# A decoder layer's long convolution: the diagonal products in three split parts, the taps split once and loaded as three arrays, the last addition on GpSimd

## What is computed

```
kv[i,j,l]  = ctx[i,l] * ctx[j,l]                       (l = 0..511, 36 pairs i<=j)
y[i,j,l]   = sum over m<=l of taps[h,l-m] * kv[i,j,m]  + D[h] * kv[i,j,l]
out[j,l]   = sum over i of y[i,j,l] * q[i,l]           (q = normalised x, transposed)
```

## Time and profile before

| | us |
|---|---|
| median of 3 runs (2049.78 to 2053.88) | 2050.71 |
| the profiled execution | 2049.21 |
| its span in the profile | 2047.4 |
| PE busy in the span | 1961.0 (96%) |
| DVE busy | 1565.9 (76%) |
| ACT busy | 929.3 (45%) |
| POOL busy | 781.7 (38%) |
| granted TensorE clock, mean | 0.991 |

### The profile page before, as it was taken

The page is one execution under the profiler, slowest core; times in us unless marked ns, Lnnn a source line. Parts: engine busy times, 40 slices in busy tenths (PEclk is TensorE's granted clock), DMA queues, the critical chain, the costliest instruction groups (busy, mean ns, idle before and its releaser), DMA issues.

```text
span 2047.4 us, 44848 instructions
## 1 busy us (share of the span) xinstructions
PE 1961.0 (96%) x15500; PEld 1607.5 (79%) x15500; DVE 1565.9 (76%) x5012; ACT 929.3 (45%) x3481; POOL 781.7 (38%) x883
## 2 busy tenths in 40 slices
PE   6899999999999989989999999999998999999899
PEld 6788888888888867778888888888886677777687
DVE  5777777777777767667777777777776899999887
ACT  4554545555455544445555455545553222222233
POOL 4444433334333323323333232233331554555454
PEclk8999999999999999999999999999999999999999
DMA  5156111111111221111111111111114633332243
GB/s 209 42 131 138 60 56 53 53 73 53 53 63 63 84 87 60 63 42 53 53 53 53 53 53 56 60 53 53 53 52 152 173 98 87 90 90 85 98 147 121
DMA packets 71538, 162.20 MB, mean 79 GB/s; under 512 B 6656, under 2 KB 15232, under 8 KB 71184
## 3 DMA queue, kind: packets, MB, share of 16 engines
q1 hardware_dynamic: 62720, 142.48, 20.7%
q0 software_dynamic: 3840, 8.39, 2.2%
q10 hardware_dynamic: 4752, 8.46, 1.1%
HBM read 108.96 MB, written 50.41 MB: 78 GB/s over the span
## 4 chain that ended last, share of the span: by engine, by line
PE 76%; DVE 15%; issue 4%; ACT 3%; POOL 1%; DVEq 0%; DMA 0%; ACTq 0%; POOLq 0%
PE banks L528 21%; PE banks L590 15%; PE banks L543 9%; PE banks L1131 8%; PE banks L567 8%; PE banks L553 5%; PE banks L1337 4%; PE banks L521 4%; DVE terms L1163 2%; DVE m L854 2%; DVE pr L878 2%; DVE banks L1177 2%; DVE banks L1173 1%; ACT pr L664 1%; DVE terms L1180 1%
## 5 line engine op out<-in xcount | busy, mean ns | idle before, releaser
L664 ACT ACTIVATE pr<-pr,mx 128x128 f32<-128x128 f32 x1024 | 398.9, 391 | 419.7 <-DVE mx L878 419.7
L739 POOL TENSOR_TENSOR m<-m,rope_sb 128x512 f32<-128x512 f32 x160 | 206.9, 1293 | 522.3 <-ACT m L651 522.3
L528 PE MATMUL banks<-xTh,wh 128*128 128x256 f32 x1280 | 378.2, 295 | 2.9 <-DVE xTl L838 1.4
L528 PE MATMUL banks<-xTl,wh 128*128 128x256 f32 x1280 | 364.7, 285 | 0.0
L528 PE MATMUL banks<-xTh,wl 128*128 128x256 f32 x1280 | 364.4, 285 | 0.0
L1131 PE MATMUL banks<-kv,tap 128*128 128x288 f32 x1280 | 323.9, 410 | 12.7 <-DVE res L1187 10.9
L1131 PEld LDWEIGHTS banks<-kv,tap 128*128 128x128 f32 x1280 | 238.1, 190 | 98.1 <-issue 36.5
L528 PEld LDWEIGHTS banks<-xTh,wh 128*128 128x128 f32 x1280 | 248.1, 194 | 5.5 <-issue 2.7
L528 PEld LDWEIGHTS banks<-xTl,wh 128*128 128x128 f32 x1280 | 248.3, 194 | 0.0
L528 PEld LDWEIGHTS banks<-xTh,wl 128*128 128x128 f32 x1280 | 247.8, 194 | 0.0
L887 DVE TENSOR_TENSOR den<-ac,es 128x4 f32<-128x4 f32 x256 | 53.0, 207 | 251.8 <-ACT es L667 251.6
(11 more groups left out here) (110 smaller groups left out, 3840.1 us busy)
## 6 DMA issues: line engine op xcount, KB each, us to landing
tap<-padded_taps SPq DMA_DIRECT2D x64, 256.0 KB, 3.3
kk<-in_ctxt SPq DMA_DIRECT2D x64, 192.0 KB, 3.4
x_in<-in_x SPq DMA_DIRECT2D x16, 512.0 KB, 3.8
xt_split<-xTh SPq DMA_DIRECT2D x16, 512.0 KB, 2.6
xt_split<-xTl SPq DMA_DIRECT2D x16, 512.0 KB, 3.6
xb<-in_x SPq DMA_DIRECT2D x16, 512.0 KB, 4.5
factors<-in_factors POOLq DMA_DIRECT2D x8, 1024.0 KB, 8.6
x_part_rows<-x SPq DMA_DIRECT2D x16, 512.0 KB, 3.0
```

What stands on the lines that cost most here:

```text
L528: last = pe.matmul(bank[:, h * T:(h + 1) * T], w[:, n, c, h * P:(h + 1) * P], a[:, s, c, :], start=(c == 0 and i == 0), stop=(c == KD - 1 ...
L664: act.activation(pr[:, s, a, cols], pr[:, s, a, cols], ACT.Exp, bias=mx[:, s, i:i + 1], scale=-1.0, accum_out=ac[:, s, i:i + 1])
L739: pool.tensor_tensor(m2[:, s], m2[:, s], rope_sb[:, 1 if i == 0 else 0, 1:3], ALU.mult).then_inc(sin_ready, 1)
```

## The change

The four diagonal matmuls of a unit become twelve of type float32r, on split operands; the six below the diagonal stay float32. This holds from unit 2 on (`split(u)`); units 0 and 1 stay as they are. The taps are split once, during the attention, into a high and a low part, and DRAM scratch holds three arrays (whole, high, low). A unit loads three tap arrays: the whole one without its last block (128 x 384), and high and low (128 x 512 each). kv's first block is split in the unit, the high part by ACT, the low part by POOL. DVE's last addition goes to POOL. PE now waits for `one_added` in place of `res_ready`, DVE for `res_ready` of unit u-2. The buffer `pr` of the attention moves into the shared arena, where the convolution's high and low taps later lie.

```diff
     def load(sp, u):
         bg, h, s = where(u)
         wait(sp, kv_ready, u - 1)
         sp.dma_start(kk[:, s], ctx_in[bg, h]).then_inc(kk_landed[s], 16)
         wait(sp, conv_done, u - 1)
-        sp.dma_start(tap[:, s], bass.AP(tensor=pad_dram.tensor, offset=h * PADW, ap=[[1, P], [1, D]]))\
-          .then_inc(tap_landed[s], 16)
+        whole = D - P if split(u) else D
+        sp.dma_start(tap[:, s, 0:whole], diagonals(0, h, whole)).then_inc(tap_landed[s], 16)
+        if split(u):
+            for i, part in ((1, tap_hi), (2, tap_lo)):
+                sp.dma_start(part[:, s].bitcast(F32), diagonals(i, h, D)).then_inc(tap_landed[s], 16)
...
+    def diagonals(i, h, columns):
+        return bass.AP(tensor=pad_dram.tensor, offset=(i * CH + h) * PADW, ap=[[1, P], [1, columns]])
...
     def first_loads(sp):
-        sp.wait_ge(tap_out, 16)
+        sp.wait_ge(tap_out, 48)
...
+    def pairs_high(act, u):
+        act.wait_ge(kv_ready, u + 1)
+        act.copy(kv_hi[:, u % 2], kv[:, u % 2, 0, :]).then_inc(kv_hi_ready, 1)
+
+    def pairs_low(pool, u):
+        pool.wait_ge(kv_hi_ready, u - 1)
+        pool.tensor_tensor(kv_lo[:, u % 2], kv[:, u % 2, 0, :], kv_hi[:, u % 2].bitcast(F32),
+                           ALU.subtract).then_inc(kv_lo_ready, 1)
+
+    def last_sum(pool, u):
+        n, s = CD * BG, u % 2
+        pool.wait_ge(one_added, u + 1)
+        wait(pool, res_placed, u - 1)
+        pool.tensor_tensor(res[:, s], terms[:, s, :, n:2 * n], terms[:, s, :, 2 * n:3 * n], ALU.add).then_inc(res_ready, 1)
+
     def gpsimd(pool):
-        for u in range(2, NCU):
-            pairs(pool, u)
+        for u in range(NCU):
+            if u + 2 < NCU:
+                pairs(pool, u + 2)
+                pairs_low(pool, u + 2)
+            last_sum(pool, u)
...
         for u in range(NCU):
             if 1 <= u < NCU - 1:
                 fetch(act, u + 1)
+            if u + 2 < NCU:
+                pairs_high(act, u + 2)
             place(act, u)
...
     def products(pe, u):
         s = u % 2
-        pe.wait_ge(tap_landed[s], 16 * (u // 2 + 1))
+        pe.wait_ge(tap_landed[s], 16 + 48 * (u // 2))
         pe.wait_ge(kv_ready, u + 1)
-        wait(pe, res_ready, u - 1)
+        wait(pe, kv_lo_ready, u - 1)
+        wait(pe, one_added, u - 1)
         for d in range(KD):
+            block = slice(d * P, (d + 1) * P)
             for c in range(d, KD):
-                last = pe.matmul(y[:, s, c, 0:NY], tap[:, s, d * P:(d + 1) * P], kv[:, s, c - d, :],
-                                 start=(d == 0), stop=(d == c))
+                if c == d and split(u):
+                    for n, (a, b) in enumerate([(tap_hi, kv_hi), (tap_hi, kv_lo), (tap_lo, kv_hi)]):
+                        last = pe.matmul(y[:, s, c, 0:NY], a[:, s, block], b[:, s], start=(d == 0 and n == 0), stop=(n == 2))
+                else:
+                    last = pe.matmul(y[:, s, c, 0:NY], tap[:, s, block], kv[:, s, c - d, :],
+                                     start=(d == 0), stop=(d == c))
...
             dve.wait_ge(qs_ready, u + 1)
+            wait(dve, res_ready, u - 1)
             dve.wait_ge(conv_done, u + 1)
...
-            dve.tensor_tensor(y[:, s, :, 3 * n:4 * n], tt[:, :, 0:n], y[:, s, :, 2 * n:3 * n],
+            dve.tensor_tensor(tt[:, :, 2 * n:3 * n], tt[:, :, 0:n], y[:, s, :, 2 * n:3 * n],
                               ALU.add).then_inc(one_added, 1)
-            dve.wait_ge(one_added, u + 1)
-            wait(dve, res_placed, u - 1)
-            dve.tensor_tensor(res[:, s], tt[:, :, n:2 * n], y[:, s, :, 3 * n:4 * n], ALU.add).then_inc(res_ready, 1)
```

In the attention part and the mix:

```diff
@@ SP, first body
-            sp.dma_start(tap0[:, 0:1], ssm_pad[:, P - 1:P], allow_slow_non_contiguous=True).then_inc(tap_in, 16)
-            sp.dma_start(tap0[:, 1:2], dcoef).then_inc(tap_in, 16)
-            sp.dma_start(pad_dram, ssm_pad).then_inc(tap_in, 16)
+            sp.dma_start(taps[:], ssm_pad).then_inc(tap_in, 16)
+            sp.dma_start(through[:], dcoef).then_inc(tap_in, 16)
@@ SP, later bodies
-            if y.number == 1:
-                sp.wait_ge(tap_added, 1)
-                sp.wait_ge(tap_in, 48)
-                sp.dma_start(pad_dram[:, P - 1:P], tap0[:, 0:1], allow_slow_non_contiguous=True).then_inc(tap_out, 16)
+            if y.number == 2:
+                sp.wait_ge(tap_lo, 1)
+                for i, part in enumerate((taps[:], tap_h[:].bitcast(F32), tap_l[:].bitcast(F32))):
+                    sp.dma_start(pad_dram[i], part).then_inc(tap_out, 16)
@@ ACT
+                if y.number == 1 and p == 0:
+                    act.wait_ge(tap_added, 1)
+                    act.copy(tap_h[:], taps[:]).then_inc(tap_hi, 1)
@@ POOL
                 if y.first and p == 7:
-                    pool.wait_ge(tap_in, 48)
-                    pool.tensor_tensor(tap0[:, 0:1], tap0[:, 0:1], tap0[:, 1:2], ALU.add).then_inc(tap_added, 1)
+                    pool.wait_ge(tap_in, 32)
+                    pool.tensor_tensor(taps[:, P - 1:P], taps[:, P - 1:P], through[:], ALU.add).then_inc(tap_added, 1)
+                if y.number == 1 and p == 2:
+                    pool.wait_ge(tap_hi, 1)
+                    pool.tensor_tensor(tap_l[:], taps[:], tap_h[:].bitcast(F32), ALU.subtract).then_inc(tap_lo, 1)
@@ mix, PE
-                    pe.wait_ge(res_ready, NBG * CH - 1)
+                    pe.wait_ge(one_added, NBG * CH - 1)
...
-                    pe.wait_ge(res_ready, NBG * CH)
+                    pe.wait_ge(one_added, NBG * CH)
@@ decoder_layer
-    pad_dram = nc.dram_tensor("padded_taps", [CH, PADW], F32).ap()
+    pad_dram = nc.dram_tensor("padded_taps", [3, P, TW], F32).ap()
```

More of the change, by code:

```diff
@@ L48 @@
 PADW = P + D
+TW = CH * PADW // P
 Programs = namedtuple("Programs", "sync tensor scalar gpsimd vector")
@@ L97, in __init__ @@
         self.fsum = self.tables + 6 * T + 2 * GS * HD
-        words = self.fsum + KD * D
+        self.probs = self.fsum + KD * D
+        self.pairs = self.probs + 8 * T
+        words = self.pairs + 4 * NY
         ctx.enter_context(nc.sbuf_tensor("arena", [P, words], F32))
@@ L148, in attention_part @@
     vv = sb("vv", [P, 2, NT, GS * HD])
-    pr = sb("pr", [P, 4, 2, T])
+    pr = space.at("pr", space.probs, 4, 2, T)
     mx = sb("mx", [P, 4, 2 * NT])
@@ L164, in attention_part @@
     rs2 = sb("rs2", [P, NT])
-    tap0 = sb("tap0", [CH, 2])
+    taps = sb("taps", [P, TW])
+    tap_h = sb("tap_h", [P, TW], F32R)
+    tap_l = sb("tap_l", [P, TW], F32R)
+    through = sb("through", [P, 1])
     sP = space.banks[:, 0:GS]
@@ L187, in attention_part @@
     tap_added = sem("tap_added")
+    tap_hi = sem("tap_hi")
+    tap_lo = sem("tap_lo")
     x_landed = sem("x_landed")
@@ L1004, in conv_part @@
 def conv_part(nc, ctx, space, ctx_in, pad_dram, q2_dram, x1t_stored, qk_done, v_done, m_ready, sin_ready, v_ready, qr_ready,
-              masked, pt_masked, ot_lo, out_done, x1_ready, x1t_evac, tap_out, res_ready, res_placed):
+              masked, pt_masked, ot_lo, out_done, x1_ready, x1t_evac, tap_out, one_added, res_ready, res_placed):
     def sem(name):
@@ L1014, in conv_part @@
     terms = space.at("terms", space.moving + 5632, 2, KD, 5 * 8 * BG)
+    tap_hi = space.at("conv_tap_hi", space.probs, 2, D, dt=F32R)
+    tap_lo = space.at("conv_tap_lo", space.probs + 2 * D, 2, D, dt=F32R)
+    kv_hi = space.at("kv_hi", space.pairs, 2, NY, dt=F32R)
+    kv_lo = space.at("kv_lo", space.pairs + 2 * NY, 2, NY, dt=F32R)
     big = space.queries
@@ L1022, in conv_part @@
     kv_ready = sem("kv_ready")
+    kv_hi_ready = sem("kv_hi_ready")
+    kv_lo_ready = sem("kv_lo_ready")
     qs_ready = sem("qs_ready")
@@ L1027, in conv_part @@
     two_added = sem("two_added")
-    one_added = sem("one_added")
     NCU = NBG * CH
@@ L1043, in projected, with split @@
         eng.wait_ge(v_done, NV)
+    def split(u):
+        return u >= 2
+    def diagonals(i, h, columns):
+        return bass.AP(tensor=pad_dram.tensor, offset=(i * CH + h) * PADW, ap=[[1, P], [1, columns]])
     def load(sp, u):
@@ L1182, in vector, with mix_part @@
             dve.wait_ge(two_added, u + 1)
-            dve.tensor_tensor(y[:, s, :, 3 * n:4 * n], tt[:, :, 0:n], y[:, s, :, 2 * n:3 * n],
+            dve.tensor_tensor(tt[:, :, 2 * n:3 * n], tt[:, :, 0:n], y[:, s, :, 2 * n:3 * n],
                               ALU.add).then_inc(one_added, 1)
-            dve.wait_ge(one_added, u + 1)
-            wait(dve, res_placed, u - 1)
-            dve.tensor_tensor(res[:, s], tt[:, :, n:2 * n], y[:, s, :, 3 * n:4 * n], ALU.add).then_inc(res_ready, 1)
     Conv = namedtuple("Conv", "first_loads first_pairs first_queries first_products sync tensor scalar gpsimd vector")
     return Conv(first_loads, first_pairs, first_queries, first_products, sync, tensor, scalar, gpsimd, vector)
-def mix_part(nc, ctx, space, x1_dram, bias, out, x1_stored, out_done, qk_done, qr_ready, f_in, res_ready, res_placed):
```

(10 more changed lines are left out.)

## The result

Before 2051.36 us (median of 4 runs, 2049.78 to 2053.88), after **2090.78 us** (4 runs, 2087.56 to 2100.83). The ratio is 1.0199, with a 95% interval of 1.0162 to 1.0237: slower by 2%. The forecast was 2060.4 with a range of 2030 to 2088, so the side was right, the size was four times as large as forecast, and the time lies just outside the range, next to the second rival's 2094.

A forecast was written before the change was run, and what follows sets the result against it. PE and DVE, both nearly full, bound the convolution at 5.235 us a unit. 53 periods at 5.33 (+5.0), eight at 5.79 (+4.4), start and end (+0.3) gave +9.7 on 2049.21; set to the median, 2060.4 us, range 2030 to 2088.

The forecast's parts named there:

- second rival: Convolution's tap loads: slow reads pile up at 135 GB/s, 5.76 us a unit, 2094 us in all; chance 0.19.
- the landing of the three tap loads: Convolution: a unit's three tap arrays land in 5.85 us, bounds 4.4 to 6.7, extra bytes at 180 GB/s.
- The units with query loads: Convolution units 4 to 11, queries loaded behind the taps: landing 6.75 us, 5.79 us a unit, +4.4 us together.
- The start: Convolution's unit 2: ACT's copy and POOL's low part come before PE's first matmul, +1.2 us (0 to 2).
- The end: Last two units of the convolution: DVE loses its last addition, -0.9 us.
- the form of the loop: Convolution: tap landing, 0.08, then 4.74 us of matmuls make up two units, giving 5.33 us a unit.
- PE's part: PE's matmuls in a convolution unit fall from 5.12 to 4.74 us: eight float32 records go, twelve float32r matmuls come.
- POOL's 4.87: POOL's work in a convolution unit, including its stop for ACT: 4.87 us, just over PE and DVE's 4.82.
- DVE's 4.67: DVE's work in a convolution unit up to what PE waits for, last addition gone: 4.67 us.
- third rival: Convolution: float32r matmuls of 288 columns cost as much as 512, 5.42 us a unit, 2062 us; chance 0.03.
- first rival: Convolution: taps land in time, under 5.4 us; POOL sets the pace at 4.87 a unit, 2030 us; chance 0.36.
- pile-up: Convolution: slow tap reads pile up at 135 GB/s, 5.76 us a unit, 2094 us; chance 0.19.

## Why the prediction was wrong in size

*The step that failed* is the landing of the three tap loads. The prediction took 180 GB/s for the 459 kB on top of one load's 3.3 us, between rows at 161 and 202 of the earlier trace rows; the change shows 459/(6.3 - 3.3) = 153, below either of them. The row at 202 had kk's packets mixed in, which are not slow, and the argument that three arrays lie in three places and so relieve each other found no support: two loads land after 4.8, three after 6.3. Only the row at 135, beside a query load, was lower. The packets show why the rows of the kernel before were too kind: one of 2 KB took 0.129 us there, where one tap load stands alone, and 0.183 to 0.185 where two or three follow each other. With 6.3 the prediction's own formula gives (6.3 + 0.08 + 4.74)/2 = 5.56 a unit; measured are 5.64. That is 50 times 0.3 us, half of the whole miss.

*The units with query loads* were set at 5.79 and took 6.24. The waits show taps and kk in turn. The DMA issues of the changed kernel, 1605 to 1655 us:

```profile
conv_tap_lo<-padded_taps SPq DMA_DIRECT2D x8, 256.0 KB, 6.1
...
kk<-in_ctxt SPq DMA_DIRECT2D x8, 192.0 KB, 6.9
```

The taps are there 0.84 + 6.1 us after the first issue, for 6.75 assumed, but kk lands 6.9 us after its own issue, and POOL's chain behind it (pairs, ACT, low part) then holds PE at times. "If the taps hold the queue up, kk is late as well, but then the tap loop is longer anyway" was wrong for these eight units.

*The start* was set at +1.2 and cost 5.4. The prediction looked at POOL's and ACT's new steps there and not at the taps. The changed kernel, first matmul of unit 2:

```profile
1597.41 0.61 PE L1184 MATMUL banks<-kv_hi,conv_tap_hi 128*128 128x288 f32 x1 [4.33 <-DMA conv_tap_lo<-padded_taps]
```

SP issued the first of the three loads at 1588.79, so they took 8.6 us. Unit 2 starts 4.1 us later than before (1597.41 for 1593.31), 1.0 of it from the attention; the other 3.1 are a part of the 5.4 us. The remaining 2.3 are PE's: unit 2 takes it 7.39 us up to SP's next issue at 1604.80, for 5.12 before. Behind the 4.33 us without work the granted clock is at its lower level (1.2 GHz, 0.50), while the kernel before has 1.00 there; columns as in the earlier trace rows:

```profile
1597.00:1600.00 3.00, 2.59 (x7) 2.17 (x8) 0.82 (x2) 0.64 (x2) 2.08 (x1) 0.50 0.84 290
1600.00:1605.00 5.00, 5.00 (x21) 4.08 (x21) 0.10 (x1) 1.80 (x4) 2.15 (x5) 0.72 0.01 2
```

From 1600 to 1640 us it is 0.92 on the mean (1.00 before), so the units with queries have a part of it too. No step had counted the clock. *The end* was set at -0.9 and cost 4.6: units 62 and 63 still wait for their taps, and the mix starts with PE at a granted clock of 0.80 (1960 to 1985 us; 0.89 in the like stretch before).

*What held.* Two tap-bound units need landing plus 4.8 us of PE: the form of the loop was right. PE's part: 4.74 forecast, from 1700.91 to SP's next issue at 1705.71 4.80. POOL's 4.87 was a little too long: without the tap loads a unit takes 4.86, and POOL waits 0.16 of it in about half of the units. The low part 0.80 and the last sum 0.73, as computed from other shapes: 0.80 and 0.73 (mean 796 and 725 ns). DVE's 4.67 and the loop of 5.01: shown by the last addition alone. The float32r matmuls are not dear; the third rival is out. Its price of 2062 was wrong, though: PE does every unit, so 5.93 of matmuls would be 5.93 a unit and not 5.42, 61 x 0.695 = 42 us more, about 2093. The time alone wouldn't have told it from what happened; PE's 4.80 does. The first rival's mechanism is real, but only if the reads are spread: 2030 without taps, 2036 to 2039 with rows apart. The formula of the Trainium skill, page "DMA: Bandwidth & Descriptors", section "Anatomy of one DMA", that backed it (an estimate of 3.65 us for 721 kB) is met by no landing here; the nearest is 4.5 us, for three DMAs from rows apart. The second rival is what happened in the main: it had 5.76 a unit (5.64 measured) and 2094. That its time is so near is luck in part: it had too much in the steady units and the ones with queries (7.1 a unit, for 6.24), and nearly nothing for start and end, which cost 11.0 us with the first +1.0.

*The chances.* Slower had 0.49 and was right. The pile-up had 0.19, though both rows that were read as the taps' own (161, and 135 beside a query load) lay below the rate that was taken. Where a term is unknown and two loops meet near it, the middle of its bounds isn't the likeliest value; it should have gone by the row with nothing but taps, and even that one (L = 6.15) is a little short, as it comes from one load and not from three in a row.

## What to carry to other kernels

A load that reads nearly the same few kilobytes for all partitions (a Toeplitz matrix cut from one row) is cheap only while it is hidden: ask how much slack it has before tripling it, and price it from a stretch in which only such loads are in flight. When two engines are in step with each other, take from the one that is easier to relieve and measure it alone: here one addition moved to an engine with slack gave 14 us, and the larger part of the change gave it back nearly four times over. A pattern whose slowest dimension is short takes a DMA off most of its engines: with two groups the kernel took 2665 us. And before a part is made faster, ask what stands just behind it: with the split, PE, DVE and POOL all have limits between 4.7 and 4.9 us a unit, and the moved addition alone already gives 5.01, so the split had little to give even with fast loads.

## What the runs showed that was not expected

- Rows 132 bytes apart, overlapping nearly wholly in 19 KB, read as fast as rows with no overlap; rows 4 bytes apart in 2.5 KB don't: 2036.96 against 2090.78 us. With a copy for each group rows 4 bytes apart do as well: 0.111 us a packet, for 0.183.
- Odd starts cost nothing: 2036.40 against 2038.56.
- With patterns of three dimensions every issue on SP takes 0.5 to 0.6 us, kk's plain one too (0.59, for 0.43).
- Two groups in the slowest dimension: 2665 us, DMA engines at 0.17.
